# Layer 2 of a relational graph network on three bf16 pieces of each node row, and the edge count of layer 1 with 10 weight columns, ahead of a tile's sums

## The chip, the cores and the metric

The kernel runs on one core of a Trainium2 chip. A core has five engines that run their own instruction streams and meet at semaphores: TensorE (PE; its weight loads are shown apart as PEld), VectorE (DVE), ScalarE (ACT), GpSimd (POOL) and SyncE (SP, which issues DMAs). The metric is the time of one execution on the device, in microseconds (us); less is better.

## What is computed

Two layers of a relational graph convolution over 12500 nodes with 128 channels and 200000 edges sorted by their target, then a residual and a normalisation of each row. An edge's type, one of 10, is the argmax of ten of its attributes. For each target and type the source rows are averaged, and each average goes through the type's own 128x128 matrix.

```python
def _rgcn_layer(x, src, dst, edge_type, w_rel, root, bias):
    N = x.shape[0]
    seg = dst * NUM_REL + edge_type
    xs = x[src]
    sums = jax.ops.segment_sum(xs, seg, num_segments=N * NUM_REL)
    cnt = jax.ops.segment_sum(jnp.ones(seg.shape, x.dtype), seg, num_segments=N * NUM_REL)
    mean = (sums / jnp.maximum(cnt, 1.0)[:, None]).reshape(N, NUM_REL, -1)
    return jnp.einsum('nrd,rdo->no', mean, w_rel) + x @ root + bias
...
edge_type = jnp.argmax(msg[:, NODE_EMB_DIM:-NODE_EMB_DIM], axis=1).astype(jnp.int32)
h = jax.nn.relu(_rgcn_layer(x, src, dst, edge_type, w_rel1, root1, b1))
return _rgcn_layer(h, src, dst, edge_type, w_rel2, root2, b2)
...
x = _layernorm(x + _L0_gnn_ref(...), axis=-1)
```

## The kernel before

**Tiles.** An edge tile is 128 edges, one per partition. Eight tiles are an *octet*, four are a *quad*, seven octets are a *half*. A layer is 28 halves (the last one is shorter), each of which also ends a block of 448 nodes. So a layer has 28 x 7 octets, 391 quads and 1563 tiles.

**Rows.** POOL gathers the source rows of a tile with one indirect DMA (line 1379): 128 rows of 128 fp32 values, 512 B each, from `x` in layer 1 and from the table `htab` in DRAM in layer 2. They land in `rows`, which has room for seven octets. Ahead of each octet's eight gathers POOL waits for `agg_ready[o]` of the half before (line 1412): the products must have read the octet's old rows.

**Sums.** DVE writes a 0/1 matrix `S` for an octet (`make_S`, line 2103; two buffers, 1600 columns: 8 tiles x 10 types x 20 targets). PE multiplies (`aggregate`, lines 1760 to 1770): a product with zeros opens the bank of a quad, then for each tile `rows` are the weights and 10 x 13, 16, 18 or 20 columns of `S` the moving side. Both are fp32, and the profile shows two passes, each with its own weight load, for one such product. In layer 1 a bf16 product of `hit_typ` and `hit` follows each tile's sums; it counts the edges by type. Its weights are 128 columns of `hit_typ`, of which the first 10 are the tile's own; its output has 128 partitions, of which 10 are used. The last product of an octet raises `agg_ready[o]`. DVE then adds the bank into `ring` (`add_sums`, line 2116).

**A block's end.** One half later, between the octets, the block that is complete is divided by its counts (`reciprocals`, `spread` on PE, `scale` on DVE, line 2160), goes through the ten matrices (`transform`, line 1829), gets its bias on ACT (`take_out`), is turned back on PE (`turn_back`, line 1837, raises `back_turned`), and ACT copies it out as rows (`take_rows`, line 1627, raises `h_ready`). In layer 1 SP writes these rows to `htab` (`save_part`); in layer 2 DVE adds `x` and normalises (`centre`, lines 2173 to 2178, in octet 5; `spread_of`; `normalise`).

**Order.** The order on each engine is written out by hand in the loops over halves and octets. In DVE's, iteration `o` holds `make_S(o + 1)`, a part of the block's end, and `add_sums(o)`. Layer 1 also makes the next half's types (`make_types` in octet 2, `take_types` in octet 6). The last block of a layer is done in two parts, EARLY (192 nodes) and LATE (212).

**Between the layers** POOL waits until every row of `htab` is written (`rows_saved`). After the last gather of layer 2 some four octets and the last block remain.

## Time and profile before

| | |
|---|---|
| median of 3 runs | 4696.83 us (4691.28 to 4699.89) |
| the profiled execution, its own time | 4687.58 us |
| its span, first to last instruction | 4685.9 us |
| POOL busy | 2994.9 us, 64% |
| PE busy / PE weight loads | 2460.3 us, 53% / 1795.0 us, 38% |
| DVE busy | 1878.4 us, 40% |
| ACT busy | 365.3 us, 8% |
| mean granted TensorE clock | 0.716 of full |

No engine is busy all the time; the engines' idle times and what ends them have to be read beside the busy ones. A wait that is put down to "remote" ended with a semaphore for which the profile has no instruction that ended just then.

### The profile page before, as it was taken

Reading aid. Unit: us, or ns where it says so; the run is one execution under the profiler, and the core shown is the slowest. Engines: PE = TensorE matmul, PEld = TensorE weight load, DVE = VectorE, ACT = ScalarE, POOL = GpSimd, SP = SyncE. Lnnn points to the kernel's source line nnn. Section 1 sums busy time; section 2 is a strip of 40 time slices with the busy share of each in tenths; the row PEclk is TensorE's granted clock in tenths of the full one; section 3 lists DMA queues with packets and bytes.
Section 4 is the critical chain, followed back from the end, with each engine's and each line's share of the span. In section 5 each row is a group of like instructions: output and inputs, shape, how many; then the busy total and the mean of one; then the engine's idle time right before and its main releaser. Section 6 shows DMA issues by size and latency. Waiting matters only on the chain.

```text
span 4685.9 us, 32483 instructions
## 1 busy us (share of the span) xinstructions
PE 2460.3 (53%) x10851; PEld 1795.0 (38%) x10852; DVE 1878.4 (40%) x2158; ACT 365.3 (8%) x397; POOL 2994.9 (64%) x3139
## 2 busy tenths in 40 slices
PE   3556566655656655565724454454445454544446
PEld 2344344443434444443523333333333333333334
DVE  4444444444444344444513333333333333333334
ACT  1001000010100001010100000010100000000100
POOL 7666666666666666666356666666666666666662
PEclk8677677676767667676766677777767676777777
DMA  4222222222222222222111222121212222221221
GB/s 117 61 62 80 62 65 75 63 79 61 80 62 63 77 61 79 63 74 57 41 48 49 55 53 56 51 59 52 56 53 56 54 55 54 56 56 52 56 55 34
DMA packets 147439, 285.98 MB, mean 61 GB/s; under 512 B 61147, under 2 KB 81711, under 8 KB 143824
## 3 DMA queue, kind: packets, MB, share of 16 engines
q0 software_dynamic: 100032, 205.07, 16.7%
q1 hardware_dynamic: 42604, 79.64, 5.2%
q10 hardware_dynamic: 4759, 0.73, 0.1%
q8 instruction: 21, 0.34, 0.0%
q14 instruction: 23, 0.19, 0.0%
HBM read 263.37 MB, written 21.85 MB: 61 GB/s over the span
## 4 chain that ended last, share of the span: by engine, by line
another core or an unknown queue 47%; DVE 20%; PE 18%; issue 11%; DVEq 3%; ACT 1%; DMA 0%; ACTq 0%; SPq 0%
PE ps_agg L1765 8%; DVE S L2103 6%; PE ps_out L1829 5%; DVE ring L2116 5%; DVE mean L2160 2%; DVE z_end L2141 2%; PE ps_bc L1783 2%; DVEq L2215 2%; PE ps_agg L1760 1%; DVEq L2112 1%; DVE hit L2097 1%; ACT ring L1596 1%; PE ps_out L1824 1%; DVEq L2116 0%
## 5 line engine op out<-in xcount | busy, mean ns | idle before, releaser
L1379 POOL DMA_INDIRECT rows<-table,idx_s x1563 | 1486.0, 951 | 841.2 <-issue 457.2
L1379 POOL DMA_INDIRECT rows<-in_x_dram,idx_s x1507 | 1449.1, 962 | 765.9 <-issue 446.9
L1765 PE MATMUL ps_agg<-S,rows 128*128 128x130 f32 (+3 forms) x6256 | 1527.2, 384 | 275.6 <-issue 274.6
L1765 PEld LDWEIGHTS ps_agg<-S,rows 128*128 128x128 f32 x6256 | 1239.9, 239 | 494.1 <-issue 415.1
L2116 DVE TENSOR_TENSOR ring<-ps_agg,ring 128x429 f32 (+1 forms) x782 | 456.3, 584 | 1889.0 <-remote 1459.0
L2103 DVE TENSOR_TENSOR S<-ps_iota,comb_b 128x1600 f32<-128x1600 f32 x392 | 712.5, 1818 | 108.4 <-issue 106.7
L1760 PE MATMUL ps_agg<-zero_b 128*128 128x429 bf16 (+1 forms) x782 | 321.9, 412 | 742.6 <-issue 385.5
L1783 PE MATMUL ps_bc<-rc_b,sel 74*128 74x448 bf16 x540 | 203.0, 469 | 908.3 <-DVE mean L2160 516.7
L2160 DVE TENSOR_TENSOR mean<-ps_bc,ring 128x896 f32<-128x896 f32 (+2 forms) x284 | 300.9, 1061 | 751.0 <-remote 692.3
L1829 PE MATMUL ps_out<-mean,wall 128*128 128x448 f32 (+1 forms) x1120 | 550.4, 620 | 55.9 <-DVE mean L2160 40.2
L1760 PEld LDWEIGHTS ps_agg<-zero_b 128*128 128x128 bf16 x782 | 88.8, 114 | 877.3 <-issue 628.5
L1783 PEld LDWEIGHTS ps_bc<-rc_b,sel 74*128 74x128 bf16 x540 | 44.6, 112 | 967.7 <-DVE mean L2160 541.8
L1829 PEld LDWEIGHTS ps_out<-mean,wall 128*128 128x128 f32 x1120 | 242.5, 223 | 248.3 <-issue 185.9
L1770 PE MATMUL ps_agg<-hit,hit_typ 128*128 128x13 bf16 (+3 forms) x1564 | 294.8, 189 | 71.1 <-issue 70.7
L1596 ACT COPY ring<-zero_f 128x4928 f32<-128x4928 f32 (+1 forms) x54 | 231.9, 4294 | 55.1 <-DVE mean L2160 53.2
L1770 PEld LDWEIGHTS ps_agg<-hit,hit_typ 128*128 128x128 bf16 x1564 | 180.3, 115 | 92.4 <-issue 92.0
L1590 ACT COPY idx_s<-idx_t 128x32 uint32 (+1 forms) x110 | 23.3, 212 | 2437.9 <-remote 1919.9
L1837 PE MATMUL ps_out<-ident,outT 128*112 128x128 f32 x216 | 44.5, 339 | 103.8 <-ACT outT L1617 76.5
L2141 DVE RECIPROCAL z_end<-z_s 10x448 f32<-10x448 f32 (+2 forms) x29 | 82.2, 2835 | 1.0
L1837 PEld LDWEIGHTS ps_out<-ident,outT 128*112 128x112 f32 x216 | 30.8, 192 | 116.7 <-ACT outT L1617 85.0
L1824 PE MATMUL ps_out<-xt_s,root 128*128 128x448 f32 (+1 forms) x112 | 74.6, 759 | 0.0
L1379 POOL DMA_INDIRECT rows<-in_x_dram,idx_t x48 | 48.5, 1011 | 14.6 <-issue 14.6
(148 smaller groups left out, 645.2 us busy)
## 6 DMA issues: line engine op xcount, KB each, us to landing
attr<-in_edge_attr_dram SPq DMA_DIRECT2D x27, 1176.0 KB
rows<-table,idx_s POOLq DMA_INDIRECT x1563
rows<-in_x_dram,idx_s POOLq DMA_INDIRECT x1507
x_in<-in_x_dram SPq DMA_DIRECT2D x54, 224.0 KB
table<-h_s SPq DMA_DIRECT2D x27, 224.0 KB
table<-outT SPq DMA_DIRECT2D x27, 224.0 KB
xt_s<-table SPq DMA_DIRECT2D x27, 224.0 KB
out_dram<-h_s SPq DMA_DIRECT2D x27, 224.0 KB
```

Of the source, the lines that this page charges most:

```text
L1379: pool.indirect_dma_start(out=rows[:, o, j, :], out_offset=None, in_=(x, htab)[l][:, :], in_offset=bass.IndirectOffsetOnAxis(ap=at, axis=0 ...
L1596: a_.copy(ring[:, :, lo:lo + n], zero_f[:, 0:1].rearrange("p (a u) -> p a u", a=1) .to_broadcast([P, R + 1, n])).then_inc(ring_zeroed, 1)
L1760: t_.matmul(bank[:, 0:used], lhsT=zero_b[:, 0:P], rhs=zero_b[:, 0:used], start=True, stop=False)
L1765: ins = t_.matmul(sums[:, :, lo:lo + w], lhsT=rows[:, o, jj, :], rhs=S[:, (par + o) % 2, jj, :].rearrange("p (r n) -> p r n", n=WN)[:, :, ...
L1770: ins = t_.matmul(bank[:, R * QWIN + lo:R * QWIN + lo + w], lhsT=hit_typ[:, par, t * R:t * R + P], rhs=hit[:, par, t, 0:w], start=False, s ...
L1783: ins = t_.matmul(ps_bc[:, c, 0:HN], lhsT=sel[:, 2 * k + c, :], rhs=rc_b[:, 0:HN], start=True, stop=True)
L1824: t_.matmul(bank[:, 0:n], lhsT=root[l][:, :], rhs=xt_s[:, lo:lo + n], start=True, stop=False).then_inc(root_done, 1)
L1829: ins = t_.matmul(bank[:, 0:n], lhsT=wall[l][:, r, :], rhs=mean[:, r, lo:lo + n], start=False, stop=(r == R - 1))
L2103: v_.tensor_tensor(S[:, sl, :, :], bc1(ps_iota[:, 0:TCOL], GT, TCOL), bc(comb_b[:, par, o * GT:(o + 1) * GT], GT, TCOL), ALU.is_equal).the ...
L2116: v_.tensor_tensor(win, ps_agg[(par + o) % 2][:, h, 0:planes * QWIN] .rearrange("p (r n) -> p r n", n=QWIN), win, ALU.add).then_inc(added[ ...
L2141: v_.reciprocal(f1, f0).then_inc(rc_step[1], 1)
L2160: v_.tensor_tensor(mean[:, 2 * k:2 * k + 2, lo:lo + n], counts, ring[:, 2 * k:2 * k + 2, par * HN + lo:par * HN + lo + n], ALU.mult).then_ ...
```

## The change

In layer 2 the rows in `htab` become three bf16 pieces: the value rounded to bf16, the rest rounded to bf16, and the rest of that, 384 values or 768 B for 512 B. ACT's `take_rows` writes the first piece, a new DVE helper `pieces` the two others; `h_ready` moves from ACT to DVE. A gather of layer 2 fetches all three; `S` is written in bf16 there, and a tile's sums are three bf16 products for one fp32 product. In layer 1 the count's product takes the tile's own 10 weight columns and stands ahead of the tile's sums. To make room, some constants and `hit` move into memory of other tiles; `SyncE`'s saves read the new tiles.

```diff
@@ gather (POOL), tables
-                    out=rows[:, o, j, :], out_offset=None, in_=(x, htab)[l][:, :],
+                    out=(rows_x, rows_h)[l][:, o, j, :], out_offset=None, in_=(x, htab)[l][:, :],
...
+        rows_h = sb("rows_h", [P, OCTS, GT, 3 * C], BF16)
+        rows_x = rows_h[:, :, :, 0:2 * C].bitcast(F32)
+        S_x = sb("S_x", [P, 2, GT, TCOL])
+        S_h = S_x[:, :, :, 0:TCOL // 2].bitcast(BF16)
...
-        htab = table2[0:N, :]
+        htab = table2[0:3 * N // 2, :].rearrange("r c -> (r c)").bitcast(BF16).rearrange("(n d) -> n d", d=3 * C)
@@ take_rows (ACT)
-                    a_.copy(blocks(to, n).rearrange("p c d -> p (c d)"), bank[0:p, 0:c * C]).then_inc(h_ready, 1)
+                    a_.copy(blocks(to, n)[:, :, 0:C], bank[0:p, 0:c * C].rearrange("p (c d) -> p c d", c=c)
+                            ).then_inc(h_piece[0], 1)
@@ aggregate (PE)
-                        ins = t_.matmul(sums[:, :, lo:lo + w], lhsT=rows[:, o, jj, :],
-                                        rhs=S[:, (par + o) % 2, jj, :].rearrange("p (r n) -> p r n", n=WN)[:, :, 0:w],
-                                        start=False, stop=(j == 3 and l == 1))
                         if l == 0:
                             t = o * GT + jj
-                            ins = t_.matmul(bank[:, R * QWIN + lo:R * QWIN + lo + w],
-                                            lhsT=hit_typ[:, par, t * R:t * R + P], rhs=hit[:, par, t, 0:w],
-                                            start=False, stop=(j == 3))
+                            t_.matmul(bank[0:R, R * QWIN + lo:R * QWIN + lo + w],
+                                      lhsT=hit_typ[:, par, t * R:(t + 1) * R], rhs=hit[:, par, t, 0:w],
+                                      start=False, stop=False)
+                        at = (S_x, S_h)[l][:, (par + o) % 2, jj, :].rearrange("p (r n) -> p r n", n=WN)[:, :, 0:w]
+                        for k in range((1, 3)[l]):
+                            ins = t_.matmul(sums[:, :, lo:lo + w],
+                                            lhsT=(rows_x, rows_h)[l][:, o, jj, k * C:(k + 1) * C], rhs=at,
+                                            start=False, stop=(j == 3 and k == (0, 2)[l]))
@@ DVE
+                def pieces(b, n, made, to, rest, bank=ps_out):
+
+                    to, rest = blocks(to, n), blocks(rest, n)
+                    p, c, _ = rest.shape
+                    dve.wait_ge(h_piece[0], made)
+                    hold(b)
+                    v_.tensor_tensor(rest, bank[0:p, 0:c * C].rearrange("p (c d) -> p c d", c=c), to[:, :, 0:C],
+                                     ALU.subtract).then_inc(h_piece[1], 1)
+                    dve.wait_ge(h_piece[1], made)
+                    v_.tensor_copy(to[:, :, C:2 * C], rest).then_inc(h_piece[2], 1)
+                    dve.wait_ge(h_piece[2], made)
+                    v_.tensor_tensor(to[:, :, 2 * C:3 * C], rest, to[:, :, C:2 * C], ALU.subtract
+                                     ).then_inc(h_ready, 1)
...
                             if last and o == 4:
 
-                                if l == 1:
+                                if l == 0:
+                                    pieces(END - 1, HN, past, h3_s, h_s)
+                                else:
                                     centre(END - 1, HN, END, END - 1, past, (x_in_done, before * 16))
...
+                            if l == 0 and some and o == 5 and not last:
+                                pieces(b - 1, HN, past, h3_s, h_s)
+                            if l == 0 and last and o == 4:
+                                pieces(END, EARLY, end, h3_early, rest_end)
...
                     if l == 0:
+                        pieces(END, LATE, late, h3_late, rest_end, late_back)
```

PE in layer 1, the first quad of a half, before: a tile's sums (`S`, `rows`) and then its count (`hit`, `hit_typ`).

```order
L1760 MATMUL ps_agg<-zero_b 128x429
L1765 MATMUL ps_agg<-S,rows 128x10x13
L1770 MATMUL ps_agg<-hit,hit_typ 128x13
L1765 MATMUL ps_agg<-S,rows 128x10x16
L1770 MATMUL ps_agg<-hit,hit_typ 128x16
```

The same place after (`nat_d` is where `hit` now lies).

```order
L1770 MATMUL ps_agg<-zero_b 128x429
L1777 MATMUL ps_agg<-nat_d,hit_typ 10x13
L1782 MATMUL ps_agg<-S_x,rows_h 128x10x13
L1777 MATMUL ps_agg<-nat_d,hit_typ 10x16
L1782 MATMUL ps_agg<-S_x,rows_h 128x10x16
```

The count now comes first and writes 10 partitions; the last product of an octet, which raises `agg_ready`, is a product of the sums.

PE in layer 2, the first quad of a half, before and, in the second fence, after.

```order
L1760 MATMUL ps_agg<-zero_b 128x390
L1765 MATMUL ps_agg<-S,rows 128x10x13
L1765 MATMUL ps_agg<-S,rows 128x10x16
L1765 MATMUL ps_agg<-S,rows 128x10x18
L1765 MATMUL ps_agg<-S,rows 128x10x20
```

```order
L1770 MATMUL ps_agg<-zero_b 128x390
L1782 MATMUL ps_agg<-S_x,rows_h 128x10x13 x3
L1782 MATMUL ps_agg<-S_x,rows_h 128x10x16 x3
L1782 MATMUL ps_agg<-S_x,rows_h 128x10x18 x3
L1782 MATMUL ps_agg<-S_x,rows_h 128x10x20 x3
```

Four fp32 products of two passes each have become twelve bf16 products.

DVE in layer 1, octets 5 and 6 of a half in the loop, before.

```order
L2103 TENSOR_TENSOR S<-ps_iota,comb_b 128x1600
L2116 ISA
L2116 TENSOR_TENSOR ring<-ps_agg,ring 128x11x39
L2116 ISA
L2116 TENSOR_TENSOR ring<-ps_agg,ring 128x11x39
L2093 SCALAR_TENSOR_TENSOR comb_b<-ps_bc,rel_t 128x56
L2095 TENSOR_TENSOR hit_typ<-ps_bc,rev_r 128x560
L2097 TENSOR_TENSOR hit<-ps_iota,rel_t 128x1120
L2103 TENSOR_TENSOR S<-ps_iota,comb_b 128x1600
```

The same place after.

```order
L2115 TENSOR_TENSOR S_x<-ps_iota,comb_b 128x1600
L2128 ISA
L2128 TENSOR_TENSOR ring<-ps_agg,ring 128x11x39
L2128 ISA
L2128 TENSOR_TENSOR ring<-ps_agg,ring 128x11x39
L2200 TENSOR_TENSOR h_s<-ps_out,h_s 112x512
L2203 CAST h_s<-h_s 112x4x128
L2205 TENSOR_TENSOR h_s<-h_s 112x4x128
L2105 SCALAR_TENSOR_TENSOR comb_b<-ps_bc,rel_t 128x56
L2107 TENSOR_TENSOR hit_typ<-ps_bc,rev_r 128x560
L2109 TENSOR_TENSOR nat_d<-ps_iota,rel_t 128x1120
L2115 TENSOR_TENSOR S_x<-ps_iota,comb_b 128x1600
```

Three instructions of `pieces`, of which the first waits for ACT, stand between the additions of octet 5 and the types and the `S` of the next half.

## Rows read from the trace of the kernel before

**Rows 1.** POOL: groups by line; busy us, mean ns | idle before, its releasers.
```profile
L1379 POOL DMA_INDIRECT rows<-table,idx_s x1563 | 1486.0, 951 | 841.2 <-issue 457.2 <-remote 305.3 <-DMA table<-z_end 69.0
L1379 POOL DMA_INDIRECT rows<-in_x_dram,idx_s x1507 | 1449.1, 962 | 765.9 <-issue 446.9 <-remote 299.5 <-PE ps_agg L1770 19.5
```
**Rows 2.** POOL's waits, whole span: releaser: us in total, times, longest.
```profile
POOL rows L1379 <- remote: 604.9, 152, 11.4
```
**Rows 3.** Timeline of POOL in layer 2: start, us, instruction [idle before].
```profile
3357.59 0.95 POOL L1379 DMA_INDIRECT rows<-table,idx_s  x1 [5.19 <-remote]
...
3369.49 0.95 POOL L1379 DMA_INDIRECT rows<-table,idx_s  x1 [2.20 <-PE ps_agg L1765]
```
**Rows 4.** The same, later: the gathers behind a long wait.
```profile
3404.27 0.94 POOL L1379 DMA_INDIRECT rows<-table,idx_s  x1 [4.61 <-remote]
...
3439.05 0.95 POOL L1379 DMA_INDIRECT rows<-table,idx_s  x1 [5.00 <-remote]
...
3462.62 0.94 POOL L1379 DMA_INDIRECT rows<-table,idx_s  x1 [3.21 <-remote]
...
3508.66 0.94 POOL L1379 DMA_INDIRECT rows<-table,idx_s  x1 [5.92 <-remote]
```
**Rows 5.** Timeline of all engines around one such wait.
```profile
3378.50 1.30 PE L1765 MATMUL ps_agg<-S,rows 128*128 128x130 f32 x8
...
3403.60 1.26 DVE L2116 TENSOR_TENSOR ring<-ps_agg,ring 128x390 f32 x2 [16.78 <-remote]
```
**Rows 6.** Timeline of PE in layer 2: a quad at full clock.
```profile
3374.43 0.33 PE L1760 MATMUL ps_agg<-zero_b 128*128 128x390 bf16 x1
...
3374.59 1.30 PE L1765 MATMUL ps_agg<-S,rows 128*128 128x130 f32 x8
...
3375.73 0.33 PE L1760 MATMUL ps_agg<-zero_b 128*128 128x390 bf16 x1
```
**Rows 7.** The same at half clock.
```profile
3386.95 0.50 PE L1760 MATMUL ps_agg<-zero_b 128*128 128x390 bf16 x1 [7.15 <-issue]
...
3387.25 2.44 PE L1765 MATMUL ps_agg<-S,rows 128*128 128x130 f32 x8
...
3389.49 0.53 PE L1760 MATMUL ps_agg<-zero_b 128*128 128x390 bf16 x1
```
**Rows 8.** Windows: engines' busy us (x instructions), PEclk, DMA share, GB/s.
```profile
3373.00:3379.00 6.00, 5.20 (x38) 4.88 (x37) 2.86 (x3) 0.84 (x2) 4.54 (x5) 1.00 0.22 55
3387.00:3392.00 5.00, 4.88 (x18) 4.39 (x18) 0.00 (x0) 0.00 (x0) 3.78 (x5) 0.56 0.21 52
```
**Rows 9.** Timeline of layer 1 around octet 0 of a half.
```profile
1128.63 0.95 POOL L1379 DMA_INDIRECT rows<-in_x_dram,idx_s  x1 [3.79 <-remote]
...
1131.27 1.82 DVE L2103 TENSOR_TENSOR S<-ps_iota,comb_b 128x1600 f32<-128x1600 f32 x1
...
1139.17 0.58 PE L1817 MATMUL ps_out<-ident,x_in 112*128 112x112 f32 x4
```
**Rows 10.** Groups by line and form: prices of DVE, and weight loads.
```profile
L2173 DVE TENSOR_TENSOR z_s<-ps_out,x_in 112x512 f32<-112x512 f32 x27 | 18.4, 681 | 1.6 <-PE ps_out L1837 1.6
...
L2143 DVE CAST rc_b<-z_end 10x448 bf16<-10x448 f32 x27 | 11.9, 439 | 0.9
...
L1770 PEld LDWEIGHTS ps_agg<-hit,hit_typ 128*128 128x128 bf16 x1564 | 180.3, 115 | 92.4 <-issue 92.0
```
**Rows 11.** A gather beside DVE in the timeline.
```profile
3384.39 0.69 DVE L2178 SCALAR_TENSOR_TENSOR z_s<-stat,z_s 112x512 f32<-112x512 f32 x1
3384.51 1.39 POOL L1379 DMA_INDIRECT rows<-table,idx_s  x1 [0.30 <-issue]
```
**Rows 12.** Timeline between the layers.
```profile
2325.57 0.38 PE L1817 MATMUL ps_out<-ident,x_in 96*128 96x96 f32 x2 [0.68 <-ACT h_s L1627]
...
2326.64 0.82 PE L1795 MATMUL ps_bc<-rc_b,sel 74*128 74x192 bf16 x4 [0.51 <-DVE rc_b L2150]
...
2361.75 0.94 POOL L1379 DMA_INDIRECT rows<-table,idx_s  x1 [69.00 <-DMA table<-z_end]
```

More of the change, by code:

```diff
@@ L1195, in gnn_kernel @@
         back_turned = sem("back_turned")
+        h_piece = [sem(f"h_piece{k}") for k in range(3)]
         h_ready = sem("h_ready")
@@ L1262, in gnn_kernel @@
         idx_s = sb("idx_s", [P, 2, HT], U32)
-        rows = sb("rows", [P, OCTS, GT, C])
-        S = sb("S", [P, 2, GT, TCOL])
+        rows_h = sb("rows_h", [P, OCTS, GT, 3 * C], BF16)
+        rows_x = rows_h[:, :, :, 0:2 * C].bitcast(F32)
+        S_x = sb("S_x", [P, 2, GT, TCOL])
+        S_h = S_x[:, :, :, 0:TCOL // 2].bitcast(BF16)
         comb_b = sb("comb_b", [P, 2, HT])
-        hit = sb("hit", [P, 2, HT, WN], BF16)
+        hit = nat_d[:, :, :].rearrange("p k c -> p (k c)")[:, 0:HT * WN].bitcast(BF16) \
+            .rearrange("p (u t n) -> p u t n", u=2, n=WN)
         hit_typ = sb("hit_typ", [P, 2, HT * R + P], BF16)
@@ L1274, in gnn_kernel @@
         rc_m = sb("rc_m", [R, HN], BF16)
-        rising = mean[:, :, :].rearrange("p r n -> p (r n)")[:, 0:CHUNKS * P].rearrange("p (k c) -> p k c", c=P)
+        mean_f = mean[:, :, :].rearrange("p r n -> p (r n)")
+        rising = mean_f[:, 0:CHUNKS * P].rearrange("p (k c) -> p k c", c=P)
+        row_u = mean_f[0:1, CHUNKS * P:CHUNKS * P + 3 * QUADS]
+        half_row, lap_row, low_row, high_row = (
+            mean_f[0:1, CHUNKS * P + k * QUADS:CHUNKS * P + (k + 1) * QUADS] for k in range(3, 7))
         wall = [sb(f"wall{l}", [P, R, C]) for l in range(2)]
@@ L1283, in gnn_kernel @@
         h_s = sb("h_s", [NH, 4, C])
+        h3_s = sb("h3_s", [NH, 4, 3 * C], BF16)
         z_s = sb("z_s", [NH, 4, C])
@@ L1512, in _ @@
                         save_counts(b - 1, before)
-                        save_part(b - 1, 0, HN, before, h_s)
-                save_part(*EARLY_PART, PARTS - 1, h_early)
-                save_part(*LATE_PART, PARTS, z_end)
+                        save_part(b - 1, 0, HN, before, h3_s)
+                save_part(*EARLY_PART, PARTS - 1, h3_early)
+                save_part(*LATE_PART, PARTS, h3_late)
                 save_counts(END, PARTS)
@@ L1679, in _ @@
                                 take_out(l, b - 1, 0, HN, None if is_(b, 1) else prev, past, saved)
-                                take_rows(b - 1, HN, past, saved, h_s)
+                                take_rows(b - 1, HN, past, saved, h3_s)
                             else:
@@ L1695, in _ @@
                         take_out(l, *EARLY_PART, None, early, None)
-                        take_rows(END, EARLY, early, None, h_early)
+                        take_rows(END, EARLY, early, None, h3_early)
                         clear(0, HN, early - 1)
                         take_out(l, *LATE_PART, None, late, None, late_out)
-                        take_rows(END, LATE, late, None, z_end, late_back)
+                        take_rows(END, LATE, late, None, h3_late, late_back)
                         clear(1, ENDN, late)
@@ L2098, in take_types, with make_S @@
                                      bc(rel_t[:, cols], HT, WN), ALU.is_equal).then_inc(typ_taken, 1)
-                def make_S(par, o, used, sl):
+                def make_S(l, par, o, used, sl):
                     if used is not None:
                         dve.wait_ge(used[0], used[1])
-                    v_.tensor_tensor(S[:, sl, :, :], bc1(ps_iota[:, 0:TCOL], GT, TCOL),
+                    v_.tensor_tensor((S_x, S_h)[l][:, sl, :, :], bc1(ps_iota[:, 0:TCOL], GT, TCOL),
                                      bc(comb_b[:, par, o * GT:(o + 1) * GT], GT, TCOL), ALU.is_equal
@@ L2203, in _ @@
                 dve.wait_ge(comb_ready, 1)
-                make_S(0, 0, None, 0)
+                make_S(0, 0, 0, None, 0)
                 for l in range(2):
@@ L2234, in _ @@
                                 used = (agg_ready[o - 1], with_it) if o else (agg_ready[OCTS - 1], before)
-                                make_S(par, o + 1, None if l == 0 and is_(b, 0) and o == 0 else used, sl)
+                                make_S(l, par, o + 1, None if l == 0 and is_(b, 0) and o == 0 else used, sl)
                             elif not last:
@@ L2242, in _ @@
                                 hold(b)
-                                make_S(1 - par, 0, (agg_ready[o - 1], with_it), sl)
+                                make_S(l, 1 - par, 0, (agg_ready[o - 1], with_it), sl)
                             if some and o in (1, 2, 3):
```

11 lines of the change are left out of this document (4 added, 7 removed).

## The prediction

> **What bounds the kernel now.** Start with the idle times of the engine that is busiest, not with the list of busy shares. POOL's two groups of gathers hold 1486.0 + 841.2 + 1449.1 + 765.9 = 4542.2 us of the span of 4685.9 us [rows 1]. A gather occupies POOL for 0.95 us and the next one follows 0.30 us later [rows 1, 3], so the cadence is 1.25 us, and 2 x 1563 = 3126 gathers cost 3908 us whatever the other engines do. Behind them stand 605 us of waits called "remote", 152 of them [rows 2], and 69.0 us between the layers [rows 1]. The remaining 143.7 us of the span lie before the first and behind the last of these gathers. The change has as many gathers as before, so it can shorten only the waits, the turn between the layers and the two ends.
>
> The timeline shows when the waits come: always after whole octets. From 3357.59 to 3369.49 there are (11.90 - 2.20)/1.25 = 8 gathers and then a wait of 2.2 us [rows 3]. From 3369.49 to 3404.27 there are 24 and 4.6 us, then 24 and 5.0 us, 16 and 3.2 us, 32 and 5.9 us [rows 3, 4]. A wait costs 2.2 us after 8 gathers and 5.9 us after 32: it grows by about 0.155 us for each gather, and about 1.1 us is there once per wait. So one wait after 32 gathers (5.9) is cheaper than one after 24 and one after 8 (7.0 to 7.2), or two after 16 (6.4), by 0.5 to 1.3 us. I use 1.2 us for a wait that goes away.
>
> What POOL waits for is that PE has finished an octet. PE has long finished: its last product of octet 6 ends at 3378.50 + 1.30 = 3379.80, but DVE, idle for 16.78 us, adds that octet only at 3403.60, and POOL goes on at 3404.27 [rows 4, 5]. So word of PE's end reached DVE and POOL 23.8 us late, and together. The rows don't say why. They do say that PE's own speed isn't what POOL waits for there; it matters only for how many octets are through when word gets out, that is for the number of waits.
>
> **PE in layer 2.** The bank-opening product with 390 bf16 columns takes 3374.59 - 3374.43 = 0.16 us at full clock until the next one starts, and 3387.25 - 3386.95 = 0.30 us near half clock [rows 6 to 8]: 0.42 and 0.79 ns a column. The four tiles' fp32 sums take 3375.73 - 3374.59 = 1.14 us and 3389.49 - 3387.25 = 2.24 us. The new products move three times 130 + 160 + 180 + 200 = 670 columns, 2010 in all: 0.85 us and 1.6 us, if the twelve weight loads hide. A quad then saves 0.29 us at full and 0.6 us at half clock. If they don't hide, each costs at most its recorded 115 ns [rows 10], 1.38 us for twelve, and the quad loses 0.24 us at full clock and still gains at half. I take the saving: the eight fp32 passes stream 2 x 670 columns in 1.14 us, 0.85 ns a column, just twice the 0.42 ns of bf16, so their eight loads add nothing visible. The Trainium skill ("TensorE: Matmul & The Clock Gate", Weight-path perf modes) says that a weight load of exactly 128 columns that isn't fp32 is sped up about twofold. By it twelve bf16 loads would hide under products of 54 ns and more, and the sum would be the 0.29 us; by the bare 115 ns it would be the loss. No run so far shows such loads alone.
>
> All 391 quads save 391 x (0.29 to 0.6) = 113 to 235 us of PE, nearly all of it beside POOL's cadence. What comes through is fewer waits. Layer 2 has some 73 of them (305.3 us at 4.2 us each, between the 2.2 and 5.9 of [rows 1, 3, 4]), 2.6 a half. An octet behind a restart ends about 1 us sooner. My estimate is that one wait in six goes: 12 x 1.2 = **-14.4 us**; bounds 0 and one in three, -29 us.
>
> **The tail of layer 2.** After the last gather PE's quads stand in the chain, about eight of them: two cold and six warm, 2 x 0.6 + 6 x 0.29 = 2.9 us. I take **-2.5 us** (0 to -4).
>
> **The count in layer 1.** Its weights are loaded under the pass before (115 ns, beside 1.14/8 = 0.143 us for an fp32 pass) [rows 6, 10]. Ten columns instead of 128 shorten what is hidden; the place ahead of the sums leaves as many changes between bf16 and fp32. No row shows a load of 10 columns. Bounds: all of the 115 ns saved, or as much added, on 1563 tiles, 180 us of PE either way, beside POOL's cadence; one wait in ten of layer 1 either way, 8 us. I take **0**.
>
> **`pieces` in layer 1.** Three DVE instructions per half. The first and third are priced by line 2173, 0.68 us; the cast of 512 elements by the one of 448, 0.44 x 512/448 = 0.50 us [rows 10]. With gaps 1.95 us, 26 times in the loop, 51 us of DVE. The first waits for ACT, and ACT for `back_turned`; queued behind it on DVE are the next half's types and its first `S`, for which PE waits. What hides it: after a restart at 1128.63 DVE has that `S` ready at 1131.27 + 1.82 = 1133.09, PE has octet 0 done before 1139.17 [rows 9], and POOL has 16 gathers, 20 us, before it needs it. So octet 0 has some 9 us of slack, of which 1.95 are used: **0**. Without that cover it is 51 us.
>
> **Gathers of 768 B.** A gather has the same 128 rows. The DMA engines were busy 21 to 22% where POOL ran at its full cadence [rows 8]; half as much again is a third. POOL's 1.25 us don't follow the bytes as far as any row shows: **0**, bounds 0 and the case below.
>
> **Between the layers** POOL waits for the chain of the last block, and all of `pieces` lies in it. PE turns `x` from 2325.57 while DVE still makes the reciprocals, and spreads them at 2326.64 [rows 12]. Now that turn waits for `h_ready` from DVE, which does `pieces` after the reciprocals: 1.95 + about 0.9 for the turn = 2.85 us. The early part's `pieces` (256 elements, 0.42 + 0.30 + 0.42 and gaps, 1.25 us, an estimate from the 512-wide ones) stands ahead of the last `S`, the late part's ahead of the save: 2 x 1.25. The larger save adds 0.2. Sum **+5.5 us** (4 to 8), which makes the 69.0 us some 74.5.
>
> **Sum.** -14.4 - 2.5 + 0 + 0 + 5.5 = -11.4 us. Against the profiled execution's own 4687.58 us that is 4676.2; the median of the runs lies 9.2 us above that execution, so I carry the difference to it: 4696.8 - 11.4 = **4685 us**.
>
> **Rivals.**
> *No wait goes.* The late word hides whatever PE gains; then 4696.8 + 5.5 - 2.5 = 4700 us. For it: at 3403.60 PE had been done for 24 us. Against it: 8, 16, 24 and 32 gathers between waits alternate, so something small decides.
> *Many waits go.* One in three in layer 2, some in layer 1: -29 - 8 + 3 = 4663 us. For it: the cold octets, which end last before a wait, gain most.
> *`pieces` isn't hidden (slower).* In the loop of layer 1 DVE stands at `h_piece[0]`, the next half's first `S` and its octet 0 come late. From 9 us of lateness on, each half gets another wait or the whole 1.95 us: 26 x 1.2 to 26 x 1.95 = 31 to 51 us, less the 11.4: 4716 to 4736 us. For it: word of `back_turned` from PE can be late too. Against it: octet 5's own word, which DVE needs just before, is raised behind it.
> *Bytes count.* If the growing part of a wait follows the bytes, layer 2 pays 0.5 x 0.155 x 1563 = 121 us more, 4806 us. Against it: the DMA share.
> *`pieces` slows the gathers.* A gather that overlaps a DVE instruction on two operands in SBUF took 1.39 us for 0.95 [rows 11]. Two such per half, 27 x 2 x 0.44 = 24 us, and nothing absorbed: 4709 us. The Trainium skill ("SBUF — State Buffer", Who interferes with whom) says that a copy or cast in a 2-port mode, and a two-input instruction against reads, holds ports that GpSimd needs. The trace agrees as far as this one row goes. Against it: gathers of layer 1 average 962 ns, those of layer 2 951, and yet its waits sum to the same 300 us [rows 1].
>
> **How the numbers follow.** Forecast 0.37 (own range 4670 to 4695), no wait goes 0.22, many go 0.14, `pieces` not hidden 0.14, slowed gathers 0.08, bytes 0.05. A difference under 0.2%, 9.4 us, can't be told from none here: "same" is 4687.4 to 4706.2. The forecast gives 0.23 to faster and 0.14 to same; the second case 0.17 to same, 0.03 and 0.02 to the sides; the third is faster; the rest slower, but for 0.02 of the slowed gathers. Faster 0.40, same 0.33, slower 0.27. The range for 8 in 10 reaches from the many waits to the unhidden `pieces`: 4650 to 4735; the case of the bytes stays outside.
>
> **What would show it.** Layer 2's quads at about 1.0 us for 1.3 at full clock; POOL's cadence still 1.25 us in both layers; the "remote" waits of layer 2 near 290 us in about 61 pieces, those of layer 1 unchanged at about 300 us; the wait between the layers at 74 us; DVE standing at line 2200 for less than 1 us a half. A cadence above 1.25 us in layer 2, or waits of 7 us after 24 gathers, would make me wrong by the bytes; more short waits in layer 1 by `pieces`.

## The result, and the profile after

The changed kernel takes 4754.78 us (median of 4 runs, 4753.33 to 4757.18) against 4695.81 us (4 runs), a ratio of 1.0127, 95% interval 1.0111 to 1.0143: 59 us **slower**, outside the range of 4650 to 4735. All comparisons below are ratios against the kernel before in the same session, because one and the same program takes 4657 to 4700 us in some sessions and 3998 to 4001 us in others; the last section tells what differs.

The page after: busy times, and from the 40 slices those of PE and the clock (each digit a tenth). The second fence is PE's row of the page before.

```profile
span 4751.6 us, 35733 instructions
...
PE 2899.9 (61%) x12415; PEld 1738.9 (37%) x12416; DVE 1927.0 (41%) x2245; ACT 365.7 (8%) x397; POOL 2989.0 (63%) x3139
...
PE   3877778777877777787833444444544454444545
...
PEclk9866676666767666676766776766767666666767
```
```profile
PE   3556566655656655565724454454445454544446
```

PE is busy for 2900 us, 440 us more than before, and the slices say where: seven to eight tenths in the first half of the span, which is layer 1, for five to six before, while layer 2 stands at four to five in both. The part meant to change layer 2 isn't where PE got busier.

POOL's groups, and its waits (releaser: us in total, times, longest):

```profile
L1387 POOL DMA_INDIRECT rows_h<-table,idx_s x1563 | 1484.1, 950 | 879.4 <-issue 454.9
L1387 POOL DMA_INDIRECT rows_h<-in_x_dram,idx_s x1507 | 1443.6, 958 | 800.9 <-issue 442.3
```
```profile
POOL rows_h L1387 <- remote: 598.6, 163, 10.4
POOL rows_h L1387 <- PE ps_agg L1782: 98.4, 43, 4.1
POOL rows_h L1387 <- DMA table<-z_end: 86.2, 1, 86.2
```

A gather takes 950 ns as in [rows 1], so 768 B cost POOL nothing. The "remote" waits sum to 599 us for the 605 of [rows 2], but not in the same places: 264 us in layer 1 and 335 in layer 2, where [rows 1] have 299.5 and 305.3. New are 98 us that PE itself ends, 95 of them in layer 1 (before 29, of which 19.5 in layer 1, [rows 1]), and 86.2 us between the layers for 69.0. The stages, from POOL's timeline (first gather to last of each layer; the number of waits over 1.4 us in brackets):

| us | layer 1 | between | layer 2 | rest of the span |
|---|---|---|---|---|
| before | 2288.3 (83) | 69.0 | 2258.2 (66) | 70.4 |
| after | 2319.2 (100) | 86.2 | 2277.4 (84) | 68.8 |
| difference | +30.9 | +17.2 | +19.2 | -1.6 |
| forecast | 0 | +5.5 | -14.4 | -2.5 |

**Layer 1.** A quad's weight loads, first before (with two of its products) and then after, both at full clock (start, us, instruction):

```profile
1007.44 0.10 PEld L1770 LDWEIGHTS ps_agg<-hit,hit_typ 128*128 128x128 bf16 x1
1007.55 0.30 PEld L1765 LDWEIGHTS ps_agg<-S,rows 128*128 128x128 f32 x2
1007.80 0.10 PEld L1770 LDWEIGHTS ps_agg<-hit,hit_typ 128*128 128x128 bf16 x1
1007.93 0.30 PEld L1765 LDWEIGHTS ps_agg<-S,rows 128*128 128x128 f32 x2
...
1007.93 0.17 PE L1770 MATMUL ps_agg<-hit,hit_typ 128*128 128x16 bf16 x1
1007.96 0.55 PE L1765 MATMUL ps_agg<-S,rows 128*128 128x180 f32 x2
```
```profile
1295.17 0.08 PEld L1777 LDWEIGHTS ps_agg<-nat_d,hit_typ 128*10 128x10 bf16 x1
1295.28 0.30 PEld L1782 LDWEIGHTS ps_agg<-S_x,rows_h 128*128 128x128 f32 x2
1295.74 0.08 PEld L1777 LDWEIGHTS ps_agg<-nat_d,hit_typ 128*10 128x10 bf16 x1 [0.17 <-issue]
1295.85 0.30 PEld L1782 LDWEIGHTS ps_agg<-S_x,rows_h 128*128 128x128 f32 x2
```

Before, the loader has next to no gap: 0.36 us from one tile's count to the next, and the count's load starts at 1007.80, 0.13 us ahead of its product. After, there are gaps between the loads, and the matmuls start together with them:

```profile
1294.38 0.34 PE L1770 MATMUL ps_agg<-zero_b 128*128 128x429 bf16 x1
...
1295.75 0.17 PE L1777 MATMUL ps_agg<-nat_d,hit_typ 128*10 128x18 bf16 x1
1295.85 0.57 PE L1782 MATMUL ps_agg<-S_x,rows_h 128*128 128x180 f32 x2
...
1296.90 0.34 PE L1770 MATMUL ps_agg<-zero_b 128*128 128x429 bf16 x1
```

The count's load starts at 1295.74 and its product at 1295.75; the sums' load and product both start at 1295.85. Neither load is seen to start ahead of its own product. A quad takes 1296.90 - 1294.38 = 2.52 us for 1.69, and at half clock 4.22 us for 3.28 (medians of the quads that another quad follows at once). That is 0.21 us a tile, two exposed loads of about 0.1 us: the narrow one and the wide one behind it. The single records of the tile with 180 columns put it there: from the last pass of the sums to the next count 0.25 us for 0.15, from the count to the next sums 0.10 us for 0.03. The Trainium skill says in "TensorEngine Tiling (Array Packing)", Key Properties, that "Changing tiling mode (not just tile) drains the TensorE"; the trace agrees, if a set of 10 columns counts as another mode than one of 128, which the profile doesn't say. I had not weighed that rule.

**Layer 2.** Its quads did become faster:

```profile
3374.12 0.34 PE L1770 MATMUL ps_agg<-zero_b 128*128 128x390 bf16 x1 [1.76 <-issue]
3374.30 1.09 PE L1782 MATMUL ps_agg<-S_x,rows_h 128*128 128x130 bf16 x12
3375.23 0.55 PE L1795 MATMUL ps_bc<-rc_b,sel 74*128 74x448 bf16 x2
```

From 3374.12 to 3375.23 are 1.11 us for the 1.30 of [rows 6] (1.09 in most quads; 2.10 at half clock for 2.53). The twelve products take 0.93 us, 78 ns each, less than the 97 to 115 ns of a recorded bf16 load, so the loads are hidden at least in part. The Trainium skill ("TensorE: Matmul & The Clock Gate", Weight-path perf modes) has a load of exactly 128 bf16 columns sped up about twofold; the 78 ns don't contradict it. And yet POOL waits 84 times for 66. PE's waits in 2450 to 4580 us, before and after, say what else happened:

```profile
PE ps_agg L1765 <- issue: 86.9, 74, 2.5
```
```profile
PE ps_agg L1782 <- issue: 361.5, 364, 2.5
```

"issue" is idle time ahead of a product that waited for nothing in the profile. It comes inside the sums: 74 times before, 364 times after. One such quad, while POOL gathers without a stop:

```profile
4417.73 0.33 PE L1770 MATMUL ps_agg<-zero_b 128*128 128x390 bf16 x1 [0.31 <-issue]
4419.13 0.29 PE L1782 MATMUL ps_agg<-S_x,rows_h 128*128 128x130 bf16 x2 [1.08 <-issue]
4419.86 0.27 PE L1782 MATMUL ps_agg<-S_x,rows_h 128*128 128x130 bf16 x1 [0.43 <-issue]
4421.26 0.44 PE L1782 MATMUL ps_agg<-S_x,rows_h 128*128 128x160 bf16 x2 [1.13 <-issue]
4421.99 0.30 PE L1782 MATMUL ps_agg<-S_x,rows_h 128*128 128x160 bf16 x1 [0.28 <-issue]
4424.09 0.47 PE L1782 MATMUL ps_agg<-S_x,rows_h 128*128 128x180 bf16 x2 [1.80 <-issue]
...
4426.92 0.51 PE L1782 MATMUL ps_agg<-S_x,rows_h 128*128 128x200 bf16 x2 [1.09 <-issue]
```

PE gets one or two products, then 0.3 to 1.8 us of nothing: 11 us for a quad of 1.1. I call this *crawling*. POOL's timeline beside it (its restarts after a wait):

```profile
4407.12 0.94 POOL L1387 DMA_INDIRECT rows_h<-table,idx_s  x1 [3.75 <-remote]
...
4430.56 0.94 POOL L1387 DMA_INDIRECT rows_h<-table,idx_s  x1 [3.73 <-remote]
```

The crawling begins some 10 us after the first restart. It ends about where POOL stands still ahead of the second: POOL's last gather before it ends at 4426.83, the last product of the quad starts at 4428.32.

### The profile page after: what moved, and what is told of

Its sections match the earlier page's. It is cut to its first block, busy times and chain, and to the rows that moved or that the text cites. A ratio compares the mean times of both kernels' runs of the same rounds, so it can differ in the third digit from the quotient of the medians.

```text
span 4751.6 us, 35733 instructions
## 1 busy us (share of the span) xinstructions
PE 2899.9 (61%) x12415; PEld 1738.9 (37%) x12416; DVE 1927.0 (41%) x2245; ACT 365.7 (8%) x397; POOL 2989.0 (63%) x3139
## 4 chain that ended last, share of the span: by engine, by line
another core or an unknown queue 40%; PE 24%; issue 16%; DVE 16%; DVEq 2%; ACT 2%; SPq 0%; DMA 0%; ACTq 0%
PE ps_agg L1782 12%; PE ps_out L1841 6%; DVE S_x L2115 5%; DVE ring L2128 4%; DVE mean L2172 2%; PE ps_bc L1795 2%; PE ps_agg L1770 1%; PE ps_agg L1777 1%; ACT ring L1604 1%; DVE z_end L2153 1%; DVEq L2241 1%; DVEq L2124 1%; PE ps_out L1836 1%; PE ps_out L1849 0%
## 5 line engine op out<-in xcount | busy, mean ns | idle before, releaser
L1782 PE MATMUL ps_agg<-S_x,rows_h 128*128 128x200 bf16 (+7 forms) x7820 | 1806.0, 358 | 438.1 <-issue 437.2
L1387 POOL DMA_INDIRECT rows_h<-table,idx_s x1563 | 1484.1, 950 | 879.4 <-issue 454.9
L1387 POOL DMA_INDIRECT rows_h<-in_x_dram,idx_s x1507 | 1443.6, 958 | 800.9 <-issue 442.3
L1782 PEld LDWEIGHTS ps_agg<-S_x,rows_h 128*128 128x128 bf16 (+1 forms) x7820 | 1109.8, 172 | 639.2 <-issue 580.4
L2115 DVE TENSOR_TENSOR S_x<-ps_iota,comb_b 128x1600 f32<-128x1600 f32 (+1 forms) x392 | 712.6, 1818 | 101.8 <-issue 100.1
L1770 PE MATMUL ps_agg<-zero_b 128*128 128x429 bf16 (+1 forms) x782 | 339.4, 434 | 413.0 <-issue 297.1
L1841 PE MATMUL ps_out<-mean,wall 128*128 128x448 f32 (+1 forms) x1120 | 563.1, 633 | 12.3 <-issue 9.7
L1777 PEld LDWEIGHTS ps_agg<-nat_d,hit_typ 128*10 128x10 bf16 x1564 | 130.2, 83 | 537.1 <-issue 516.0
L1777 PE MATMUL ps_agg<-nat_d,hit_typ 128*10 128x13 bf16 (+3 forms) x1564 | 276.7, 177 | 17.2 <-issue 16.9
L1387 POOL DMA_INDIRECT rows_h<-in_x_dram,idx_t x48 | 49.7, 1035 | 14.6 <-issue 14.6
```

The lines of the kernel that those rows point to most:

```text
L1387: pool.indirect_dma_start(out=(rows_x, rows_h)[l][:, o, j, :], out_offset=None, in_=(x, htab)[l][:, :], in_offset=bass.IndirectOffsetOnAxi ...
L1770: t_.matmul(bank[:, 0:used], lhsT=zero_b[:, 0:P], rhs=zero_b[:, 0:used], start=True, stop=False)
L1777: t_.matmul(bank[0:R, R * QWIN + lo:R * QWIN + lo + w], lhsT=hit_typ[:, par, t * R:(t + 1) * R], rhs=hit[:, par, t, 0:w], start=False, sto ...
L1782: ins = t_.matmul(sums[:, :, lo:lo + w], lhsT=(rows_x, rows_h)[l][:, o, jj, k * C:(k + 1) * C], rhs=at, start=False, stop=(j == 3 and k == ...
L1841: ins = t_.matmul(bank[:, 0:n], lhsT=wall[l][:, r, :], rhs=mean[:, r, lo:lo + n], start=False, stop=(r == R - 1))
L2115: v_.tensor_tensor((S_x, S_h)[l][:, sl, :, :], bc1(ps_iota[:, 0:TCOL], GT, TCOL), bc(comb_b[:, par, o * GT:(o + 1) * GT], GT, TCOL), ALU.i ...
```

## The experiments

Theories at the start. **A**: ten weight columns aren't loaded ahead, and layer 1 pays. **B**: it is the count's place ahead of the sums. **C**: `pieces` on DVE lengthens layer 1. For layer 2: **D**, the 768 B of a gather; **E**, the three products. The fences of edits below are shortened to what moved.

### The count alone

```diff
-  sums product of tile
-  count: lhsT=hit_typ[:, par, t * R:t * R + P], out bank[:, ...]
+  count: lhsT=hit_typ[:, par, t * R:(t + 1) * R], out bank[0:R, ...]
+  sums product of tile
```

> The kernel before with the count's product alone changed: 10 weight columns, ahead of a tile's sums. Layer 2 and the turn between the layers are as before. Theory A (ten weight columns are loaded and multiplied with nothing beside them): a layer-1 quad takes 2.5 us at full clock and 4.2 at half clock for 1.69 and 3.28, and layer 1 grows by the 31 us that the changed kernel shows: about 4727 us. Rival B (the place ahead of the sums does it): the same 4727 here, told apart by the next two kernels. Rival C (`pieces` on DVE is what lengthened layer 1): this kernel stays at 4696 us.

Measured: 4704.06 us against 4657.12, 1.0106 [1.0089, 1.0123], +47 us. Layer-1 quad 2.53 us at full clock, 96 waits there; layer 2 keeps 63 waits, and the stretch between the layers takes 80.3 us. The count alone costs most of what the whole change does; C is out as the main cause. It costs more than my 31 us: beside the kernel with 128 columns ahead (below, same session) layer 1 is 37 us longer, 2317.1 for 2279.8, and the stretch between the layers 8.5 us.

### Ten columns behind the sums

```diff
+  if l == 0 and j == 3: count (10 columns)
   sums product of tile
+  if l == 0 and j < 3: count (10 columns)
```

> The kernel before with 10 weight columns for the count, but behind the tile's sums in three of four tiles (in the fourth of a quad it stands ahead, because the last product must close all 128 partitions). Theory A (ten columns): as with the place ahead, quad 2.5 us at full clock, about 4727 us. Rival B (the place): only one tile in four is hit, quad 1.9 us, about 4703 us. Rival C: 4696 us.

4681.31 us, 1.0059 [1.0043, 1.0076]. The quad takes 2.25 us, between the 1.9 that B and the 2.5 that A expected. In this order the fourth count follows the third with the same width, so the array changes width six times a quad and not eight: 0.84 x 6/8 = 0.63 us, where 2.25 - 1.68 = 0.57 were measured. That fits A, priced by the changes of width, and not B.

### 128 columns ahead of the sums

```diff
+  count: lhsT=hit_typ[:, par, t * R:t * R + P], out bank[0:P, ...]
   sums product of tile
-  count
```

> The kernel before with the count ahead of each tile's sums, still with 128 weight columns. Theory A (ten columns): nothing is lost, quad 1.69 us at full clock, 4696 us within 10. Rival B (the place): quad 2.5 us and about 4727 us.

4659.94 us, 1.0005 [0.9995, 1.0015]; quad 1.77 us. The place costs 0.08 us a quad and no time. B is out.

### The pieces without the new count

```diff
-  count with 10 columns, ahead
+  count with 128 columns, behind, as before
```

> The changed kernel with the count as it was before (128 weight columns, behind the sums): what is left is the three bf16 pieces, the gathers of 768 B and `pieces` on DVE. Theory A: layer 1 returns to its length before, 31 us less than the changed kernel's 4755: about 4724 us, with 17 us between the layers and 17 us in layer 2 still lost. My prediction for this part alone was 4685 us. Rival C (`pieces` lengthened layer 1): 4755 us.

4676.54 us, 1.0048 [1.0032, 1.0065], +19 us, where I had predicted 11 us less. Beside the kernel with 128 columns ahead (same session): layer 1 2271.5 us for 2279.8, between the layers 75.4 for 71.8, layer 2 2257.7 for 2244.5 with 82 waits for 65. `pieces` costs nothing in layer 1, as I had worked out, and 3.6 us between the layers, somewhat under my 4 to 8. The rest of the span, 67.8 for 67.0, is the same. The loss is layer 2's.

### Bytes or products

Two kernels change one of them each. Three products on rows of 512 B:

```diff
-  htab of 3 * C bf16 a row; gather of 768 B; third product with piece k = 2
+  htab of 2 * C bf16 a row; gather of 512 B; third product with piece k = 1 again
```

> The kernel with the pieces only, but the table's rows hold two pieces, so a gather fetches 512 B as before, and the third product of a tile uses the second piece again (layer 2's sums are then not the reference's). PE does in layer 2 exactly what it does with 768 B. The kernel with the pieces only was slower than before by the ratio 1.005: 13 us in layer 2 (82 waits of POOL for 65) and some 4 between the layers. Theory D (the bytes: with longer gathers in flight PE's word of an octet's end gets stuck sooner after a restart): layer 2 falls back to 65 waits and loses the 13 us, ratio 1.001 to 1.002. Rival E (the faster or more numerous products themselves bring more waits): the ratio stays 1.005 with some 82 waits.

Rows of 768 B with one fp32 product a tile:

```diff
-  for k in range(3): product with rows_h[:, o, jj, k * C:(k + 1) * C] and S_h
+  product with rows_x[:, o, jj, :] and S_x
```

> The kernel with the pieces only, gathers of 768 B, but layer 2's sums are one fp32 product a tile as before, on the first 512 B of each row taken as fp32, with S in fp32 (its sums are then not the reference's). PE is as before, the bytes as after. Theory D (bytes): layer 2 still has some 80 waits, ratio 1.005 or more. Rival E (products): some 65 waits, ratio 1.001 to 1.002.

And two pieces, two products, 512 B:

```diff
-  for k in range(3)
+  for k in range(2)
-  v_.tensor_tensor(to[:, :, 2 * C:3 * C], rest, to[:, :, C:2 * C], ALU.subtract)
```

> Two pieces only: rows of 512 B, two bf16 products a tile, two DVE instructions in `pieces` for three. The rest of the value, below the second piece, is left out of layer 2's sums. A layer-2 quad should take 0.16 + 670 x 2 x 0.42 ns = 0.7 to 0.75 us at full clock for 1.30. Theory D (bytes): 65 waits or fewer, and PE's gain shows for the first time without the bytes: ratio 0.998 to 1.001. Rival E (the faster PE is, the more waits): ratio 1.005 or above, over 82 waits in layer 2.

The session of these three had the kernel before at 4001.22 us, and POOL never waited in either layer. Ratios: 1.0008 [0.9999, 1.0018], 1.0021 [1.0011, 1.0030], 1.0004 [0.9994, 1.0013]. Neither D nor E is told apart by them. What they show: where there are no waits, neither the bytes nor the products cost more than some 2 in 1000 (at most 1.0030, by the intervals), and `pieces` lengthens the stretch between the layers from 24.6 us (the next kernel, which has none) to 28.3 to 29.7, +4 to +5, near my +5.5. A half-clock quad of two products takes 1.48 us. Hardly any quad ran wholly at full clock, and the 1.03 us I read there is no price; in the second run of this kernel (below) two quads did, and took 0.78 us each, for the 0.7 to 0.75 I had worked out.

### Ten columns, grouped

```diff
+  if l == 0 and j == 0: the four counts of the quad, 10 columns each
   sums product of tile
-  count
```

> The kernel before with 10 weight columns for the count, the four counts of a quad together ahead of its four sums. Theory A1 (what costs is each change between a narrow and a wide set of weights: the load behind it waits until the product before it is through): two changes a quad for eight, a quad of about 1.9 us at full clock for 1.69 before and 2.53 with a count ahead of each tile; ratio 1.001 to 1.003. Theory A2 (each narrow load costs, wherever it stands): four exposed narrow loads of 0.08 to 0.1 us and one wide one, 2.1 to 2.2 us, ratio 1.005 (as with three of four behind).

0.9999 [0.9990, 1.0009], same session; run again in another, also without waits:

> The count with 10 weight columns, the four counts of a quad together ahead of its sums. Its quad was 1.70 us at full clock and 3.03 at half clock where it ran first, for 1.69 and 3.28 before. So theory A1 expects no loss where the word is late: ratio 0.998 to 1.002. Theory A2 (each narrow load costs, wherever it stands): ratio 1.005.

0.9992 [0.9983, 1.0002]. The quad takes 1.70 us at full clock (1.9 expected by A1, 2.1 by A2) and 3.03 at half, 0.25 less than before. Its loads show why (here 353.21 to 354.77):

```profile
353.51 0.14 PEld L1769 LDWEIGHTS ps_agg<-hit,hit_typ 128*10 128x10 bf16 x4 [0.20 <-issue]
353.69 1.10 PEld L1771 LDWEIGHTS ps_agg<-S,rows 128*128 128x128 f32 x8
```

Four narrow loads in a row fit in 0.14 us, and 0.04 us later the wide ones run without a gap. What costs is the change of width, twice a quad here. Both are still exposed (0.27 us from the bank's opening to the first count, where the first sums follow in 0.19 before; 0.10 us from the last count to the sums), so A1's 1.9 us missed something that the change of order gives back: with no count in between, the second pass of a tile's sums starts sooner behind the first, 0.15 us for 0.24 with 180 columns. Whether this kernel is faster where the waits exist wasn't seen; where there are none it can't be told from before.

### The whole change again

> The changed kernel once more, whole. The last four kernels ran where the kernel before takes 4001 us and POOL never waits for PE's word; the four before them where it takes 4657 us with 605 us of waits. If this run falls where the word is late, theory A and D expect the ratio 1.010 to 1.015 as recorded. If it falls where the word is prompt, every PE term is hidden beside POOL's cadence of 1.25 us and only the stretch between the layers and the tail can show: my +5.5 us and nothing for 10 weight columns, ratio 1.001 to 1.003. Rival (the narrow loads make PE itself the bound): 14 quads of 2.5 to 4.2 us a half are 35 to 59 us beside 70 us of gathers, and with the transform PE would come near the 70 us at half clock: ratio above 1.005 even there.

Beside it the kernel before took 3998.91 us, the changed one 4003.31: 1.0011 [1.0001, 1.0020]. One of its ten executions took 4897.1 us, and no trace of that one is kept. POOL's waits are down to one that matters:

```profile
POOL rows_h L1387 <- issue: 951.7, 3124, 0.3
POOL rows_h L1387 <- DMA table<-z_end: 40.2, 1, 40.2
```

PE is busy for 70% of this span and its layer-1 quads still take 2.52 us, yet both layers run at POOL's cadence. The 440 us of PE are hidden; only the stretch between the layers shows them, 40.2 us for the 24 to 25 of the grouped kernels, of which 4 to 5 are `pieces`. The rival of a PE-bound layer 1 is out where POOL never waits; where it does, 36 waits of layer 1 ended with PE's own last product (95 us).

### Which width isn't loaded ahead

```diff
-  count ahead with P columns
+  count ahead with 64 columns, and in a second kernel with 112
```

> The kernel before with the count ahead of the sums and with 64 weight columns, between the 128 that cost nothing and the 10 that cost 0.84 us a quad (the neighbouring tiles' columns come along and land in partitions that nobody uses). Theory A: if any set of weights narrower than the one before it waits until the array is through, the quad takes 2.5 us at full clock. Against that the 112-column products of the turn back are loaded ahead. If only small sets (some 32 columns or fewer) do it, the quad stays at 1.77 us, as with 128.

> The kernel before with the count ahead of the sums and with 112 weight columns. With 64 columns a layer-1 quad took 2.62 us at full clock, with 10 columns 2.53, with 128 columns 1.77. In the traces the turn back of a block loads sets of 112 fp32 columns under the product before them. Theory A in its narrow form (only sets of half the array or fewer wait): 1.77 us. Theory A in its wide form (every change between 128 columns and another width waits): 2.7 us. The time: where the kernel before takes 4000 us no difference, where it takes 4660 us about 1.011 for the wide form and 1.000 for the narrow.

With 64 columns the quad takes 2.62 us at full clock, with 112 columns 1.77. The loads at 64 and at 112:

```profile
169.62 0.11 PEld L1767 LDWEIGHTS ps_agg<-hit,hit_typ 128*64 128x64 bf16 x1 [0.17 <-issue]
169.75 0.30 PEld L1770 LDWEIGHTS ps_agg<-S,rows 128*128 128x128 f32 x2
170.25 0.10 PEld L1767 LDWEIGHTS ps_agg<-hit,hit_typ 128*64 128x64 bf16 x1 [0.21 <-issue]
```
```profile
538.73 0.13 PEld L1767 LDWEIGHTS ps_agg<-hit,hit_typ 128*112 128x112 bf16 x1
538.84 0.30 PEld L1770 LDWEIGHTS ps_agg<-S,rows 128*128 128x128 f32 x2
539.09 0.13 PEld L1767 LDWEIGHTS ps_agg<-hit,hit_typ 128*112 128x112 bf16 x1
```

Gaps at 64, none at 112: the narrow form of A. Where between 64 and 112 the boundary lies wasn't tried. In "TensorEngine Tiling (Array Packing)", Available Configurations, the Trainium skill lists 128 rows by 64 columns as a configuration of its own and none between 64 and 128 columns; the runs agree in that 112 goes with 128. The times (4006.45 us in a session with the kernel before at 3997.94; 4705.11 against a single 4699.88) are one run each and say no more.

### Bytes or products, where POOL waits

> The same kernel as the one with rows of 512 B and three products, to have it where PE's word is late (the kernel before then takes 4650 to 4700 us; the first time it ran where the word is prompt, with no wait of POOL at all and the ratio 1.001). Theory D (the bytes bring the additional waits of layer 2): 65 waits, ratio 1.001 to 1.002. Rival E (the products do): some 82 waits, ratio 1.005. Where the word is prompt again: ratio 1.001, nothing told apart.

> The same kernel as the one with rows of 768 B and fp32 products as before (layer 2's sums are made of the first 512 B taken as fp32), for the same reason. Theory D: some 80 waits in layer 2, ratio 1.005. Rival E: 65 waits, ratio 1.001 to 1.002. Where the word is prompt again: ratio 1.002.

Again no waits: 1.0004 [0.9995, 1.0014] and 1.0013 [1.0003, 1.0022]. A third time, with the two pieces beside them:

> Rows of 512 B, three products a tile (the third uses the second piece again), to have it where PE's word is late. Theory D (the bytes bring the additional waits of layer 2): some 65 waits in layer 2, ratio 1.001 to 1.002. Rival E (the products do): some 82 waits, ratio 1.005. Where the word is prompt: ratio 1.001, nothing told apart.

> Rows of 768 B with fp32 products as before (layer 2's sums are made of the first 512 B of a row taken as fp32). Theory D: some 80 waits in layer 2, ratio 1.005. Rival E: 65 waits, ratio 1.001 to 1.002. Where the word is prompt: ratio 1.002.

> Two pieces and two products a tile, rows of 512 B (what lies below the second piece is left out of layer 2's sums). Its layer-2 quad was 1.03 us at full clock, not the 0.7 to 0.75 I had worked out. Theory D (bytes), with PE's gain of 0.27 us a quad and nothing against it: 65 waits or fewer, ratio 0.998 to 1.001. Rival E (what PE gains brings more waits): over 80 waits, ratio 1.005.

No waits: 1.0006 [0.9997, 1.0016], 1.0013 [1.0003, 1.0023], 1.0002 [0.9992, 1.0011]. The last run:

> Rows of 512 B, three products a tile (the third uses the second piece again), once more to have it where PE's word is late. Kernels with fp32 products and 512 B had 63 to 69 waits of POOL in layer 2 there, the two with three products and 768 B had 82 and 84. Theory D (the bytes bring the additional waits): 63 to 69 waits, ratio 1.001 to 1.002. Rival E (the products do): some 82 waits, ratio 1.004 to 1.005. Where the word is prompt: ratio 1.001, nothing told apart.

This one had the waits, with the kernel before at 4659.4 us: 4695.63 us, 1.0077 [1.0060, 1.0094], 80 waits in layer 2, stretch between the layers 72.7 us. With 512 B the loss is all there, and if anything larger than with 768 B (1.0032 to 1.0065). So **D falls as the cause, and E holds**: the kernels with three products have 80 to 84 waits in layer 2 (three traces), those with fp32 sums 63 to 69 (five). That rests on one kernel with 512 B in one session. The fp32 sums on rows of 768 B never ran where there are waits, so a small effect of the bytes by themselves isn't excluded. With the products the form of `S` changed too, to bf16; DVE writes it in the same 1.82 us. PE's waits in 2450 to 4580 us, of this kernel, of the pieces without the new count, and of the kernel with fp32 sums and 128 columns ahead:

```profile
PE ps_agg L1777 <- issue: 304.1, 316, 2.5
```
```profile
PE ps_agg L1777 <- issue: 283.5, 304, 2.5
```
```profile
PE ps_agg L1770 <- issue: 82.4, 79, 2.5
```

The crawling goes with the products, whatever the bytes. A *gap* here means that two products of one quad start more than 0.6 us apart. In sessions without POOL's waits there is none. Where there are waits, layer 2 has 70 to 80 gaps with fp32 sums (five traces: 13 to 16 quads with three or more) and 318 to 371 with three products (three traces: 48 to 57 quads). A quad has 9 matmul records in the first case and 13 in the second. Layer 1 has had 13 all along, and with a count of 112 or 128 columns it has 244 to 280 gaps (five traces) and 83 to 92 waits, where layer 2 with fp32 sums has 63 to 69.

So the number of instructions that PE has to be given seems to count. It isn't the whole of it, for layer 1 with 10 columns has the same 13 records and far fewer gaps: 83 in the changed kernel, 98 with the count alone, 181 with ten columns behind the sums. Its quads are the slow ones (2.53 and 2.25 us for 1.68), so how long the instructions take counts as well; nor do waits follow gaps, since these three have 93 to 100. Which of the two layer 2 pays for, the higher number or the shorter products, isn't shown: no kernel here changed one alone, and the one with two products, which has the fast PE and the old number, never ran where there are waits.

## Why the prediction was wrong, point by point

**POOL's cadence** held: 1.25 us in both layers, in every kernel. (The two groups of [rows 1] hold 3070 of the 3126 gathers; the other 56 lie in my 143.7 us.)

**The price of a wait.** The 2.2 us after 8 gathers and 5.9 after 32 leave 0.95 us once per wait, not the 1.1 I wrote. The 1.2 us for one wait more or less was about right: 18 more waits cost 24 us in layer 2 of the changed kernel, 17 more cost 12 us with the pieces alone.

**The count in layer 1: 0, bounds 180 us of PE.** This step failed, and most of the loss is here. I allowed a load of 115 ns more a tile at the worst; it was 0.21 us, because the wide set behind a narrow one is exposed as well: 391 x 0.84 = 330 us of PE at full clock. I had priced the narrow load by what hid the old one, and took for granted that it could be hidden. 31 to 37 us came through in layer 1, where my bound had been 8 (one wait in ten; it was 17 more on 83 in the changed kernel, 8 more on 88 with the count alone), and 8.5 us between the layers (80.3 for 71.8), which I hadn't counted at all, though the last octets of layer 1 stand in that chain.

**`pieces` in layer 1: 0.** Right. DVE stands at line 2200 without idle time in the loop:

```profile
L2205 DVE TENSOR_TENSOR h_s<-h_s 112x512 bf16<-112x512 f32 x27 | 18.9, 699 | 0.9
...
L2200 DVE TENSOR_TENSOR h_s<-ps_out,h_s 112x512 f32<-112x512 f32 x27 | 18.4, 681 | 0.0
L2203 DVE CAST h_s<-h_s 112x512 bf16<-112x512 f32 x27 | 12.0, 443 | 0.9
```

Prices as worked out (0.68, 0.44 for 0.50, 0.70), and the kernel with the pieces alone has no longer layer 1 (2271.5 us for 2279.8).

**Gathers of 768 B: 0.** Right: 950 ns each for 951, waits of 3.50 us after 16 and 4.74 after 24 for 3.51 and 4.86 before. The case of the bytes and that of slowed gathers are out.

**PE in layer 2.** The price was nearly right (1.09 us for the 1.0 I forecast, saving 0.21 for 0.29 at full and 0.43 for 0.6 at half clock), its effect had the wrong sign: 15 to 18 waits more instead of 12 fewer, +13 to +19 us for -14.4. The step that failed is "a quad ends sooner, so fewer waits"; what the runs showed in its place is more waits, but why a faster form with more products brings them stays open. The forecast took PE's time from stretches where PE runs freely. The trace of before already had quads in which it crawls, in idle time of PE put down to "issue" that I passed over, since PE wasn't the bottleneck.

**Between the layers: +5.5.** The part I priced was nearly right (+3.6 to +5, and 1.9 us of `pieces` stand in the chain just ahead of the turn of `x`, 2366.00 to 2367.91 below); the narrow count adds 8.5 to 12. Together 86.2 for 69.0.

```profile
2366.00 0.69 DVE L2200 TENSOR_TENSOR h_s<-ps_out,h_s 112x512 f32<-112x512 f32 x1
2366.72 0.43 DVE L2203 CAST h_s<-h_s 112x512 bf16<-112x512 f32 x1
2367.18 0.69 DVE L2205 TENSOR_TENSOR h_s<-h_s 112x512 bf16<-112x512 f32 x1
...
2367.93 0.39 PE L1829 MATMUL ps_out<-ident,x_in 96*128 96x96 f32 x2 [3.76 <-DVE h_s L2205]
```

**The tail: -2.5.** Measured -1.6; too small to be told.

Every rival that I named as slower put the loss into DVE, the bytes or a port. None had PE slower in layer 1, though the bounds of the count held it: I gave it no case because both ends lay "beside POOL's cadence".

## What to carry to other kernels

Don't shrink a weight set to 10 or 64 columns between wide ones to save a load: its own load and the wide one behind it both come to the open (0.21 us a tile here). Keep it wide, or group the narrow products. Where a profile has waits put down to "remote" or "issue", an engine's own speed doesn't say what a faster form brings; look for stretches in which it is fed one instruction at a time, and don't carry the price of a free-running stretch over to them. And when a step seems hidden, check the places where its cover ends (here the turn between two layers) before writing zero.

## What the runs showed of the hardware

The same program has two conditions. In one POOL stops after one to four octets each time and waits for a word from PE that left long before ([rows 5]), 4657 to 4700 us; in the other no word is late and the program takes 3998 to 4001 us. PE then waits for rows to land (PE's waits in layer 2, second run of the grouped count):

```profile
PE ps_agg L1760 <- DMA rows<-table,idx_s: 621.9, 146, 7.2
```

The kernel before gave both on what is reported as the same chip, each steady within a session (4651 to 4664 in 13 runs, 3996 to 4007 in 31); the later sessions ran on other chips. By their time stamps two sessions with the waits came 21 and 30 minutes after the one before, the four without them 4 to 14 minutes after; whether that is the cause wasn't tried. With POOL's waits go PE's crawling and the late word; all three come together and vanish together, 650 to 700 us. What holds PE's instructions and its word back isn't in the profile, and stays open.

In the condition with waits, when PE's word got late moved too. Of PE's signals that were raised 6 to 7.5 us after a restart of POOL in layer 2, 10 of 41 came more than 0.2 us late with fp32 sums (five traces), and 75 of 97 with three products (three traces), the 512 B ones included. In layer 1, with 13 matmul records a quad in every kernel, it was 86 of 151 with a count of 112 or 128 columns (five traces) and 8 of 54 with 10 columns (three traces): there too the number isn't all.
